# Both sets of token-mixing buffers take first-layer tiles at the start and second-layer tiles at the end, with new instruction orders

## What is computed

```python
h = ln(x) * (1 + mod_1) + mod_0                 # "in"
for i in range(2):
    h = h + _time_mix(_ln(h), p[i])             # token mixing, state S_i runs along the sequence
    h = h + _channel_mix(_ln(h), p[i])          # channel mixing
x2 = x + gate_2 * ln_out(h)
hf = ln(x2) * (1 + mod_4) + mod_3
out = x2 + gate_5 * fp4_ffn(hf)                 # gate, up, down with 4-bit weights and activations
```

## Time and profile before

| | us |
|---|---|
| median of three runs | 2996.12 (2995.36 to 2997.4) |
| the profiled execution's own time | 2997.96 |
| its span, first to last instruction | 2996.1 |
| mean granted clock of PE | 0.979 of full speed |
| largest transfer queue, share of 16 engines | 3.8% |

### The profile page before, as it was taken

The page is one execution under the profiler, slowest core; times in us unless marked ns, Lnnn a source line. Parts: engine busy times, 40 slices in busy tenths (PEclk is TensorE's granted clock), DMA queues, the critical chain, the costliest instruction groups (busy, mean ns, idle before and its releaser), DMA issues.

```text
span 2996.1 us, 78846 instructions
## 1 busy us (share of the span) xinstructions
PE 2768.2 (92%) x32855; PEld 2204.0 (74%) x32855; DVE 2362.3 (79%) x5355; ACT 1380.9 (46%) x2708; POOL 1283.2 (43%) x1447
## 2 busy tenths in 40 slices
PE   6788999999999999999999999999999999999875
PEld 4567777777777777777777777777777777777653
DVE  5657888888888888888888888888888878888664
ACT  1344444544454455455455544545554454454431
POOL 3344444445444444444444444444444444444310
PEclk7899999999999999999999999999999999999997
DMA  4000000000000000000000000000000000000000
GB/s 149 14 5 9 12 12 5 9 12 12 12 12 12 5 9 12 12 13 12 12 9 9 9 12 12 12 12 9 9 9 12 12 13 12 5 9 12 8 8 7
DMA packets 36832, 41.51 MB, mean 14 GB/s; under 512 B 3273, under 2 KB 35201, under 8 KB 36481
## 3 DMA queue, kind: packets, MB, share of 16 engines
q1 hardware_dynamic: 35696, 36.32, 3.8%
q10 hardware_dynamic: 784, 0.16, 0.0%
HBM read 28.08 MB, written 8.39 MB: 12 GB/s over the span
## 4 chain that ended last, share of the span: by engine, by line
PE 59%; DVE 23%; ACT 8%; issue 6%; POOL 4%; DMA 0%; DVEq 0%; ACTq 0%; POOLq 0%
PE ps_all L1442 10%; PE ps_all L1256 9%; PE ps_all L1264 7%; PE ps_all L1456 5%; PE ps_all L1475 5%; PE ps_all L1493 5%; PE ps_all L1362 4%; DVE sxrk L1121 3%; DVE att L1127 3%; PE ps_all L1248 2%; DVE chan L1065 2%; ACT mixin L899 2%; DVE stats L1019 2%; PE ps_all L1388 2%; PE ps_all L1418 1%
## 5 line engine op out<-in xcount | busy, mean ns | idle before, releaser
L744 POOL TENSOR_TENSOR mixin<-mixin,hT_tm 128x512 f32<-128x512 f32 x320 | 389.2, 1226 | 342.9 <-DVE mixin L1086 342.8
L1442 PE MATMUL ps_all<-chan,cwk 128*128 128x256 f32 x1536 | 372.2, 389 | 8.0 <-DVE chan L1065 5.7
L1121 DVE TENSOR_TENSOR sxrk<-sxrk,dec 128x512 f32<-128x512 f32 x384 | 274.3, 714 | 105.5 <-PE ps_all L1362 101.3
L1456 PE MATMUL ps_all<-cwv,chan 128*128 128x256 f32 x1536 | 343.9, 381 | 0.0
L1442 PEld LDWEIGHTS ps_all<-chan,cwk 128*128 128x128 f32 x1536 | 282.0, 190 | 62.6 <-issue 21.8
L1456 PEld LDWEIGHTS ps_all<-cwv,chan 128*128 128x128 f32 x1536 | 290.4, 191 | 38.8 <-issue 0.3
L724 POOL TENSOR_TENSOR rstd<-var,powc 128x2 f32<-128x2 f32 x224 | 187.5, 837 | 245.8 <-DVE var L1025 244.7
L1086 DVE SCALAR_TENSOR_TENSOR mixin<-ps_all,vcol,sxrk 128x256 f32<-128x256 f32 x640 | 270.0, 476 | 11.3 <-PE ps_all L1294 4.0
L1362 PEld LDWEIGHTS ps_all<-sxrk 64*64 64x64 f32 x10240 | 170.2, 130 | 144.9 <-issue 144.8
L1362 PE MATMUL ps_all<-sxrk 64*64 64x32 f32 x10240 | 202.7, 217 | 51.2 <-DVE att L1127 48.2
L763 POOL TENSOR_TENSOR lora<-S,dec 128x256 f32<-128x256 f32 x128 | 92.8, 725 | 348.6 <-DVE S L1136 348.3
(11 more groups left out here) (187 smaller groups left out, 6270.2 us busy)
## 6 DMA issues: line engine op xcount, KB each, us to landing
xin<-in_L_attn_x_dram SPq DMA_DIRECT2D x32, 256.0 KB, 2.7
tok<-in_L_attn_x_dram SPq DMA_DIRECT2D x32, 256.0 KB, 2.7
out_dram<-x SPq DMA_DIRECT2D x32, 256.0 KB, 2.1
cwk<-in_L_attn_cWk_dram SPq DMA_DIRECT2D x2, 768.0 KB, 8.4
cwv<-in_L_attn_cWv_dram SPq DMA_DIRECT2D x2, 768.0 KB, 10.6
ffn_work<-in_L_wmod_dram SPq DMA_DIRECT2D x2, 512.0 KB, 4.3
tok<-in_L_ffn_w_down_dram SPq DMA_DIRECT2D x1, 704.0 KB, 4.3
tok<-in_L_ffn_w_gate_dram SPq DMA_DIRECT2D x1, 640.0 KB, 8.1
```

Source lines behind the costliest of these rows:

```text
L744: pool.tensor_tensor(m, m, hT["tm", l][:, :, :, 1:P + 1].rearrange("p k c t -> p (k c) t"), ALU.add).then_inc(ev["mixed"][b], 1)
L1121: v.tensor_tensor(rko, rko, t, ALU.mult).then_inc(ev["rk_lev"][b], 1)
L1442: ins = pe.matmul(bank(b, "ck", lj, "k")[:, m * TT:(m + 1) * TT], cwk[:, l, k, n:n + P], k_in[:, k, :], start=(k == 0), stop=(k == KC - 1))
L1456: ins = pe.matmul(bank(b, "cv", l, "v")[:, c * D:(c + 1) * D], relu[t // 2][:, t % 2, c * P:(c + 1) * P], cwv[:, l, t, :], start=(t == 0), ...
```

## The change

A set no longer belongs to a layer. `job(i, b)` says which tile and which layer the set b takes in its turn i, and `where(t, w)` is its inverse. Set 0 takes tile 0, then tiles 2 to 31 of layer 0, then tile 31 of layer 1; set 1 takes tile 1 of layer 0, then tiles 0 to 30 of layer 1. So tiles 0 and 1 of layer 0 are in work together at the start, and tiles 30 and 31 of layer 1 at the end. In between, turn i of set 0 is layer 0 of tile i+1 and turn i of set 1 is layer 1 of tile i-1; layer 1 thus follows one tile further behind layer 0 than before. Each set still takes 32 turns.

What follows from it in the code: the layer's weights and state are picked by `job(i, b)[1]`; where a tile's predecessor sat in the other set, ACT's `turn` copies the carried token across and waits for it; event counts are counted per turn; the second tile's input is loaded ahead into `hand[1]` by one more transfer of 256 KB. The set-up can no longer live in set 1: the raw weights, their quantised form and the modulation's left operands move to `ffn_work`, the quantisation works in place with `downT` as scratch, and its steps are placed later in the lists. `mods` is cut in two (one per sequence), each placed in the shared banks 6 and 7. The raw weights of `up` and `down` are loaded behind `mods`. The warm-up products of PE are 6 in place of 13. `ORDER`, `HEAD`, `TAIL` and `SECOND` are written anew for all engines, and `HEAD_BLOCKS` is 6 in place of 5.

```diff
@@
+    def job(i, b):
+        if b == 0:
+            return (N - 1, 1) if i == N - 1 else (i + 1 if i else 0, 0)
+        return (i - 1, 1) if i else (1, 0)
+
+    def where(t, w):
+        if w == 0:
+            return (0, 0) if t == 0 else (0, 1) if t == 1 else (t - 1, 0)
+        return (N - 1, 0) if t == N - 1 else (t + 1, 1)
...
             def cv(i, b, l):
                 if l == 0 and i > 1:
-                    emptied(pool, i - 2, 1, "wo", 1, "o")
+                    pi, pb = where(i - 2, 1)
+                    emptied(pool, pi, pb, "wo", pb, "o")
+                if l == 1 and i == 0:
+                    emptied(pool, 0, 1, "wo", 1, "o")
...
             def turn(i, b, s):
...
+                if kind == "tm":
+                    t, w = job(i, b)
+                    if t > 0:
+                        pi, pb = where(t - 1, w)
+                        past = hT["tm", pb]
+                        if pb != b:
+                            emptied(act, pi, pb, "turn", f"tm{pb}", "x")
...
-                act.activation(h[:, :, :, 0], h[:, :, :, P], ACT.Copy).then_inc(ev["carried"][b], 1)
+                act.activation(h[:, :, :, 0], past[:, :, :, P], ACT.Copy).then_inc(ev["carried"][b], 1)
...
-        raw = flat(tok[1])
-        su_norm, su_magic = flatmix[1][:, 0:IT * D], sxrk[1][:, 0:IT * D]
+        raw = [ffn_work[:, n * IT * D:(n + 1) * IT * D] for n in (2, 0, 1)]
+        su_magic = flat(downT)
...
                 if l == 0:
+                    sp.dma_start(hand[1][:, :, :], x_tiles[:, 1]).then_inc(x_loaded_beside, 16)
...
-            def mods(i, b_, _):
+            def mods(i, b_, b):
                 pe.wait_ge(mod2_loaded, 16 * KC)
-                for b in range(B):
-                    mod_rows(b, 1)
-                pe.wait_ge(mod_step, MOD_FIRST)
-                mod_rows(0, 2)
-                mod_rows(1, 2).then_inc(su_pe, 1)
+                for j, to in enumerate(SHARED):
+                    fill(pe, 0, "weights", L + 1, b, to)
+                    for k in range(KC):
+                        ins = pe.matmul(ps[to][:, :], csilu_row[b][k], wmod[k][:, (j + 1) * 2 * D:(j + 2) * 2 * D], start=(k == 0), stop=(k == KC - 1))
+                    ins.then_inc(full[to], 1)
...
-HEAD_BLOCKS, TAIL_BLOCKS = 5, 3
+HEAD_BLOCKS, TAIL_BLOCKS = 6, 3
```

580 lines of the change are left out of this document (309 added, 271 removed).

## The result

The changed kernel takes 3051.31 us (median of 4 runs, 3047.95 to 3052.74) against 2996.76 us for the kernel before on the same chip (4 runs, 2995.36 to 3000.81). The ratio is 1.0178, with a 95% interval of 1.0161 to 1.0196. I had forecast 2950 us and "faster". The measured span is 3051.0 us, 101 us above the one I had worked out.

A forecast was written before the change was run, and what follows sets the result against it. A PE-bound middle between two ends where one serial chain decides: head -4, middle -13, stretched periods -6, tail -23, in all -46 us from 2997.96, so 2952, or 2950 us against the median of 2996.12; range 2916 to 2984.

The forecast's parts named there:

- First two passes: Head, first layer: the wo additions of tile 0 near 98 us and of tile 1 at 130 us.
- my bound for the worse (44): Head: if tile 1 runs 44 us behind tile 0, tile 2 leaves the second layer at 384 us.
- Second to fourth pass of set 1: Head, tiles 0 to 2 of the second layer: ends at 206, 285 and 372 us, the last against 376.04 before (-4).
- the gain is paid out at the end: Head's term of -4 us looks like no gain, but the first layer is one tile further ahead by then.
- Middle: 27 periods between tiles 2 and 29: 86.6 us each, -13 us in all; per-period bounds 1.4 us gain, 0.5 us loss.
- headroom of up to 19 us: Mid-run period: PE's room if judged by weight loads (67.65 us) instead of matmul spans; the waits were held to speak against it.
- Stretched periods of the tail: Last periods before tile 29, 11.2 us over the nominal pace before: the new tail list wins half, -6 us.
- Tail: Everything after tile 29's second layer: 234.4 us against 257.1 before, -23 us.
- The joint phase: Tail, tiles 30 and 31 together through the second layer: 83 us, bounds 74 and 93.
- the new idle stretch: Tail, ahead of the second-last feed-forward stage: PE waits 13.7 us for its prologue, now behind dn in DVE's list.
- the one of the joint phase that is no faster and the order that closes no gap: Tail and middle: 93 instead of 83 us, 87.1 instead of 86.6 a period, total 2978 to 2990 us; chance 0.10.
- "slower" rival: Crossing at the period's end: POOL's mf.4 and tot wait for the other set's wo; 89 us periods give 3014; chance 0.06.

The follow-up runs named there:

- the run in the head: Changed kernel with GpSimd's tot ahead of the other pass's channel-mixing cv, for the second pass of set 0 and of set 1: 3057.02 us, 1.0191.

## Why the prediction was wrong

The direction was wrong and so was the size. By its own steps:

- **First two passes**: forecast 98 and 130, measured 91.7 and 136.4. Each is about right, but tile 1 came 44.7 us behind tile 0, as far as in my bound for the worse (44), for which I had named 384.
- **Second to fourth pass of set 1**: the step that failed. I forecast 76, 79 and 87 us, by dividing PE's work (71, 74 and 84 us) by the mid-run share of PE and adding a few us. The work was right at full clock (79.30 us at 0.88 are 69.8, 80.44 at 0.93 are 74.8); the share was not, and I had left out that the clock is lower here:

```profile
136.40:232.40 96.00, 79.30 (x935) 63.36 (x934) 62.30 (x127) 40.04 (x77) 35.43 (x41) 0.88 0.01 4
232.40:329.70 97.30, 80.44 (x979) 64.08 (x978) 64.05 (x142) 42.08 (x84) 39.41 (x44) 0.93 0.02 7
329.70:421.70 92.00, 85.10 (x1027) 67.04 (x1025) 72.90 (x166) 42.45 (x84) 39.55 (x45) 1.00 0.04 10
```

  These are the three passes, in the columns of the earlier trace rows. PE is busy for 79 and 80 us instead of 71 and 74, at 0.88 and 0.93 of its clock, and idle for 17 in each of the first two. Of the miss of 49.7 us (421.66 against 372), 6 are the first pass and 43 are these three. The kernel before has a stretch of the same kind, from one addition of set 1 to the next, with as many PE instructions:

```profile
203.80:286.10 82.30, 71.17 (x952) 57.63 (x952) 58.11 (x140) 37.47 (x73) 36.92 (x42) 0.96 0.03 8
```

  Its PE share is 86%, not 97%. With it my first two terms would have been 82 and 86 us; with 90 for the third, the next period of the same set before (376.04 - 286.10), the forecast of tile 2 is near 388: 12 us later than before instead of 4 earlier, but still 34 us short of the truth. The statement "the gain is paid out at the end" stood on this step. The first layer was indeed a tile further ahead, at a price that ate it. A sum of work would have warned me: up to tile 2 the kernel before has 300.95 us of PE work and 75 us of idle time. With 34 us more work, a forecast of 372 leaves 37 us of idle time, half of what there was, and I had no reason for that. Measured, it is 80.
- **What makes the 14 us between 82.3 and 96.0**, at nearly the same count and kinds of instructions, is partly told: PE's busy time is 8 us longer at the lower clock (0.88 against 0.96; times the busy time this is 69.8 and 68.3), and PE is idle for 6 us more. Its waits for the norm ahead of the channel mixing's transposes are 8.1 us instead of 1.6. That the clock is low because of such gaps fits the run that filled them. The products in the gaps gave some 5 us back and the quantisation's steps are worth 6, in the kernel before too. I tried two other orders of the first passes; both were slower. Whether a better list exists, or two first-layer chains in step cannot be packed closer, stays open.
- **Middle**: forecast 86.6 us a period and half of the stretched periods, 2344 us in all; measured 2380.7. I took "2.9 us of a period are idle" for what an order can win, and "0.5 us, a third of it the other way" for what it can lose. Two exchanges of neighbours lose 0.9. Of the 36.7 us of the miss, 30 are the steady period (27 times 1.1) and 7 the longer periods next to the ends. The size of the bound failed, and the reading below it: PE at 97% is not the only bound of a period in which 4.9 us more of VectorE work in the levels cost 3.5 to 4.6. The rule of the Trainium skill that I had weighed (Perfetto Trace Analysis, Identifying the Most-Contended Engine) was right to distrust matmul occupancy. But the headroom of up to 19 us that I had worked out by it did not show: added PE work cost 0.83 to 0.88 of its length.
- **Stretched periods of the tail**: I granted the new list half of 11.2 us. Measured, the two periods of 90.8 us are its own, and putting the steady order there took 6 us off.
- **Tail**: forecast 234.4 us, measured 248.6. The joint phase took 92.7 us instead of 83, at the upper bound I had named (93); no run tells why. The additions of tiles 30 and 31 lie 40.2 us apart and not a few, since DVE's list places tile 31's behind `dn`; PE's last products for the two end some 12 us apart (2894.2 and 2906.0). The steps behind it were right within 2.3 us each: 39.6 (38.8), 54.4 (53), 57.3 (55), 4.7 (4.6), and the new idle stretch was 13.83 us (13.7).
- **The rivals**: the one of the joint phase that is no faster and the order that closes no gap met the tail (93 us) and the part of the middle that no gap gave back. The "slower" rival had one right part, a longer steady period, at the wrong place and size: the period is 0.6 us longer, not 1.9, and GpSimd's crossing is not its cause as far as the run in the head and the waits of mid-run tell. No rival held the head, which made half of the miss. I had given it bounds of 359 to 384, with the passes behind tile 1 at PE's mid-run share.

The three misses, 49.7 + 36.7 + 14.2, are the 101 us.

## What to carry to other kernels

Cost a stage where serial chains decide by the nearest stage of the same kind in the trace, at its own busy share and its own clock, not by the share of the steady middle. An engine at 97% in a loop of in-order lists need not be its only bound: add a known amount of work to each engine in turn, at more than one place of its list, and count on slack only where the added time does not come back in the period. And when a change moves work from one end to the other, compare the busy and the idle time of both ends: the tail lost a lone chain of 72.6 us and got 8.5 us shorter, while the head, with some 34 us more of PE work in it, took 45.6 more.

## What was unexpected about the hardware

A 128x128 product on the identity in this data type shows as two records; eight of them took 2.0 us at full clock (32.4 us for 16 groups). The head is not the same from one execution to the next: with the same lists, tile 1's addition came between 134.9 and 139.4 us in eight runs, while most steady periods agree to 0.1 us. In the changed kernel's runs two or three of some twenty steady periods take 88.6 to 89.3 us instead of 87.7; in the profile of the kernel before no steady one takes more than 87.4. No run here tells why.
